# Denominators of layer 2 from pairs that GpSimd adds, and the row of maxima kept in PSUM

## The chip, the cores and the metric

The kernel runs on one core of one Trainium2 chip. The metric is the device time of one execution in microseconds (us); three runs of the kernel before took 3555.37 to 3556.21 us, median 3555.91. The engines are named as in the profile: PE is TensorE, DVE is VectorE, ACT is ScalarE, POOL is GpSimd, SP is SyncE.

## The reference

Three graph attention layers over 8192 nodes with 64 channels and one dense 0/1 adjacency matrix. Layer 0 attends over entity features, layers 1 and 2 over the features of the layer before. The core is the same in each:

```
scores = u[:, None] + v[None, :]            # one number per row, one per column
e      = where(adj > 0, leaky_relu(scores, 0.2), -9e15)
att    = softmax(e, axis=1)                 # exp(e - max), divided by its row sum
h      = elu(att @ features)
```

After layer 0 there is a residual sum and a layer norm; after layer 2 an output product over the concatenated features, a residual sum and a layer norm. So each of the 8192 x 8192 scores is made, masked, exponentiated, summed by row (the denominator) and multiplied with the features, three times over.

## The kernel before

Each layer runs over 16 blocks `b` of 512 rows. A block runs over 64 tiles `j` of 128 columns; a tile is 128 x 512 f32, with the graph's columns on the partitions. Four engines pass a tile on:

1. DVE `start_scores` (L1126) writes the score into one bank of `eps` in PSUM: `max(ua + v8, cb)`. `ua` is a row of the block, `cb` the row of maxima, both spread over the partitions in SBUF; `v8col` is one number per partition. This is called a fill below.
2. PE `mask_scores` (L736) adds -9e15 into the same bank where there is no edge. It splits the array by columns: two parts of 64 in layer 1 (`MASK_COLS`), four of 32 in layers 0 and 2, one of 128 beside other work. In layer 0 ACT fills some of the tiles.
3. ACT `probs` (L562) takes the exponential into one of 8 slots of `prob` in SBUF.
4. PE `main` (L780) adds features times probabilities of two tiles at once into bank `acc`. In layers 0 and 2 PE `denominators` (L789) also sums four tiles of `prob` at once, by a 128 x 32 matrix of ones each, into the four quarters of bank `den`. In layer 1 the denominator comes out of `acc` itself and there is no such product.

A fill of tile j waits for the exponential of the tile that had the bank: there are `ES` = 5 banks in turn. PSUM has 8 banks: five for `eps`, one each for `acc`, `den` and `misc`. `misc` takes everything else.

Every engine has its instructions in program order, written out by hand. In PE's loop over tiles the masks of `GROUP` tiles come first and then the sums of an earlier group (`LAG` groups back): 4 and 1 in layers 0 and 2, 2 and 2 in layer 1. At fixed tiles (`T_...`) stand the steps for other blocks. The tail of the block before: `T_EVAC`, `T_DEN` (ACT takes `acc` and `den` out), `T_TURN` (PE turns them), `T_A` (DVE divides), `T_EXP`, `T_B`, `T_HT`, `T_OUT`, `T_Y` (output sums and variances), `T_D` (result). The head of the next block: `T_XOR` (DVE makes edges, L974), `T_HIST` (PE counts them, L747), `T_FOLD`, `T_HEAD` (DVE finds the maxima, L992 to L1018), `T_HEADT`, `T_ROWS` (PE spreads them over the partitions in `misc`, ACT `rows_out` L623 copies them to `cb`), `T_UA` (DVE makes `ua`, L1132).

GpSimd has little to do: `tail` issues a power of -1/2 of four numbers per partition (L507, L517) and two DMAs a block (one in layer 2).

Of the kernel before, what the change touches and what calls it, by code (L numbers as in the profile page):

```python
# [46 lines left out]
GROUP = (QUAD, 2, QUAD)  # L47
LAG = (1, 2, 1)
TS = 2 * QUAD
ES = 5  # L50
AHEAD = 3
MASK_COLS = (32, 64, 32)
# [13 lines left out]
T_DEN = 5  # L66
T_TURN = 8
T_A = 13
T_EXP = 15
# [7 lines left out]
T_D = 40  # L77
# [24 lines left out]
def build(nc, x, adj, ent, W0, a0, W12, lin_w, lin_b, attn, mlp_w, mlp_b, out):  # L102
    with ExitStack() as ctx:
# [87 lines left out]
        eps = ps("eps", [P, ES, BI])  # L191
        acc = ps("acc", [P, BI])
        den = ps("den", [P, BI])
        misc = ps("misc", [P, BI])
        miscb = misc[:, :].bitcast(BF16)
# [46 lines left out]
        s_main = sem("probs_used")  # L242

# [51 lines left out]

        def freed(l, b, j):

            if j >= ES:
                return tile(l, b, j) - ES + 1
            last = max(i for i in range(NT) if i % ES == j)  # L300
            return tile(l, b, last) - NT + 1
# [181 lines left out]
        def _(pool):  # L483
# [20 lines left out]
            def tail(l, b):  # L504
                if l == 0:
                    pool.wait_ge(s_mom, blk(l, b) + 1)
                    nc.gpsimd.tensor_tensor(rstd[:, :], mom2[:, :], half[:, :], ALU.pow).then_inc(s_rstd, 1)  # L507
                if l < 2:

                    pool.wait_ge(s_oe, 4 * blk(l, b) + 4)  # L510
                    nc.gpsimd.dma_start(u_d[l + 1, bass.ds(b * BI, BI)].rearrange("(r p) -> r p", p=P),
                                        urow[:, :]).then_inc(s_ust, 16)
                    pool.wait_ge(s_y, blk(l, b) + 1)
                    nc.gpsimd.dma_start(xy_v[l, b], xin[:, :, :]).then_inc(s_x1, 16)
                else:
                    pool.wait_ge(s_mom2, b + 1)
                    nc.gpsimd.tensor_tensor(rstd[:, :], mom2[:, :], half[:, :], ALU.pow).then_inc(s_rstd2, 1)  # L517
                    pool.wait_ge(s_fin, b + 1)
                    nc.gpsimd.dma_start(out_v[b], pj[:, :, :]).then_inc(s_out, 16)

            for l in range(NLAYER):
                for b in range(NB):
                    tail(l, b)
# [3 lines left out]
        def _(act):  # L527
# [18 lines left out]
            def start_scores(l, b, j, par):  # L546

                if not (l == 0 and b == 0 and j < ES):
# [5 lines left out]
                nc.scalar.activation(eps[:, j % ES, :], ub[:, par, :], ACT.Relu, bias=v8col[:, j:j + 1],  # L554
                                     scale=1.0 - ALPHA).then_inc(s_filla, 1)

            def probs(l, b, j):

                if j % GROUP[l] == 0 and not (l == 0 and b == 0 and j < TS):
                    act.wait_ge(s_main, summed(l, b, j - TS + GROUP[l] - 1))  # L560
                act.wait_ge(s_z, tile(l, b, j) + 1)
                nc.scalar.activation(prob[:, j % TS, :], eps[:, j % ES, :], ACT.Exp,  # L562
                                     bias=v2col[:, j:j + 1]).then_inc(s_p, 1)

            def sums_out(l, b, par):
# [14 lines left out]
            def columns_out(l, b):  # L580
                act.wait_ge(s_htt, blk(l, b) + 1)
                nc.scalar.activation(ht[0:C, :], misc[0:C, :], ACT.Copy).then_inc(s_hte, 1)

            def products_out(l, b, i):

                act.wait_ge(s_om, 4 * blk(l, b) + i + 1)
                if i < 2:
                    v = misc[:, 0:2 * WC].rearrange("p (r w) -> p r w", w=WC)
# [19 lines left out]
                elif l < 2:  # L608

                    act.wait_ge(s_ust, 16 + 16 * blk(l, b))  # L610
                    nc.scalar.activation(urow[:, :], misc[0:RT, 0:P], ACT.Copy).then_inc(s_oe, 2)

            def counts_out(l, b):
                act.wait_ge(s_hist, MV * (blk(l, b) + 1))
                nc.scalar.activation(hs[:, :], misc[:, :], ACT.Copy).then_inc(s_hse, 1)  # L615

            def maxima_out(l, b, par):
                act.wait_ge(s_mt, blk(l, b) + 1)
                nc.scalar.activation(mrow[0:3, par, :], miscb[0:3, 0:BI], ACT.Copy).then_inc(s_mte, 1)  # L619
# [18 lines left out]
            for l in range(NLAYER):  # L638
                counts_out(l, 0)
                maxima_out(l, 0, 0)  # L640
                rows_out(l, 0, 0)

                def body(b, par, head, tail):
                    for t in range(NT):
# [8 lines left out]
                        if b == 0 and l == 1 and t == T_FSUM:  # L653
                            act.wait_ge(s_fs1, 1)
                            nc.scalar.activation(acc_s[0:C, 0:P], misc[0:C, 0:P], ACT.Copy).then_inc(s_fs1e, 1)
                        if b == 0 and t == T_FSUM + 4:
                            act.wait_ge(s_fsum, l + 1)
                            nc.scalar.activation(fsum[:, :], misc[:, 0:CE], ACT.Copy).then_inc(s_fsume, 1)
# [4 lines left out]
                        if head and t == T_ROWS:  # L663
# [9 lines left out]
        def _(pe):  # L673
# [9 lines left out]
            for i in range(ES):  # L683
# [40 lines left out]
            def mask_scores(l, b, j, par, cols):  # L724

                on_act = j in ON_ACT[l]
                et = eps[:, j % ES, :]
# [12 lines left out]
            def count_edges(l, b, m):  # L740
# [3 lines left out]
                for k in range(MT // 4):  # L744
                    for s in range(4):
                        j = 4 * k + s
                        mm = nc.tensor.matmul(misc[s * HB:(s + 1) * HB, :], oneh[:, m * MT + j, :],  # L747
# [5 lines left out]
            def turn_counts(l, b):  # L753
                pe.wait_ge(s_hse, blk(l, b) + 1)
                for r in range(RT):
                    mm = nc.tensor.matmul(misc[:, r * HB:(r + 1) * HB], hs[:, r * P:(r + 1) * P], fold[:, :],  # L756
# [3 lines left out]
            def feature_sum(l, j):  # L760
                if l == 1:
                    mm = nc.tensor.matmul(misc[0:C, 0:P], feat[:, 1, j, 0:C], ones[:, :], start=(j == 0),
# [4 lines left out]
                mm = nc.tensor.matmul(misc[:, 0:CE], ones[:, :], feat[:, l % 2, j, :], start=(j == 0),  # L767
# [495 lines left out]
```

## Time and profile before

| what | time |
|---|---|
| median of three runs | 3555.91 us |
| profiled execution, its own time | 3555.84 us |
| its span, first to last instruction | 3554.1 us |
| PE busy | 3220.6 us, 91% |
| DVE busy | 2877.7 us, 81% |
| ACT busy | 2261.3 us, 64% |
| POOL busy | 116.3 us, 3% |
| one block of layer 0, middle of the layer | 76.81 us |
| one block of layer 1 | 56.87 us |
| one block of layer 2 | 71.01 us |

The period of a block is the distance of two copies of `acc` (L570), which stand once in each block at the same tile. In the page's part 5 and in the grouped view, a row is a line of the kernel with its engine, operation, output and inputs, count, busy time and mean duration, and behind the second bar the idle time in front of it. Durations of consecutive instructions can overlap, so a count of instructions times their mean is more than their share of the time. One f32 matmul of the program stands as two records in the trace.

### The profile page before, as it was taken

The page shows a single profiled execution, that of the slowest core. Times are in us where ns is not written, and L with a number is a line of the kernel's source. Part 1 is how long each engine was busy: PE and PEld are TensorE (multiplying, and loading weights), DVE is VectorE, ACT ScalarE, POOL GpSimd, SP SyncE. Part 2 cuts the span into 40 slices and gives each one's busy share as a digit, 9 for nine tenths or more (in the row PEclk, how much of TensorE's full clock was granted, in tenths as well). Part 3 has the DMA queues.
Part 4 walks back from the last instruction along what each step waited for, and adds up shares of the span by engine and source line. Part 5 has one row for each costly group of instructions (what it writes and reads, how often), then busy time and mean ns, then how long its engine had stood idle before and what let it go on. Part 6 is the DMA issues. An engine that isn't in the chain of part 4 may idle for free. (4 is left out here: it accounts for less than half of the span.)

```text
span 3554.1 us, 60890 instructions
## 1 busy us (share of the span) xinstructions
PE 3220.6 (91%) x24158; PEld 1141.0 (32%) x24269; DVE 2877.7 (81%) x5283; ACT 2261.3 (64%) x3933; POOL 116.3 (3%) x138
## 2 busy tenths in 40 slices
PE   1579999999999997899999999979999999999998
PEld 0323333333333332333333333333333333333332
DVE  5468888888888875799999999976887888778876
ACT  0346666767766675577777877745656665666555
POOL 0000000000000000000000000000000000000000
PEclk9989999999999998999999999979999999999999
DMA  8999999999999941122212121211121112111200
GB/s 255 281 347 344 343 336 337 336 338 338 343 336 332 338 153 49 66 85 86 98 72 98 72 109 71 97 69 51 56 84 67 71 56 84 67 71 56 84 32 7
DMA packets 414127, 578.88 MB, mean 163 GB/s; under 512 B 294402, under 2 KB 315010, under 8 KB 389266
## 3 DMA queue, kind: packets, MB, share of 16 engines
q1 hardware_dynamic: 409458, 564.40, 49.4%
q0 software_dynamic: 4384, 10.59, 0.9%
q8 instruction: 190, 3.11, 0.3%
q14 instruction: 95, 0.78, 0.1%
HBM read 430.10 MB, written 77.69 MB: 143 GB/s over the span
## 5 line engine op out<-in xcount | busy, mean ns | idle before, releaser
L562 ACT ACTIVATE prob<-eps,v2col 128x512 f32<-128x512 f32 x3072 | 1945.5, 689 | 904.2 <-PE eps L736 894.8
L1126 DVE SCALAR_TENSOR_TENSOR eps<-ua,v8col,cb 128x512 f32<-128x512 f32 x2800 | 1975.6, 756 | 405.4 <-ACT prob L562 398.0
L780 PE MATMUL acc<-prob,feat 128*64 128x512 f32 x6144 | 1531.8, 605 | 6.7 <-ACT acc_s L570 6.7
L736 PE MATMUL eps<-nt,nbig 128*32 128x512 fp8e4 (+2 forms) x7852 | 964.6, 383 | 152.8 <-DVE eps L1126 136.3
L736 PEld LDWEIGHTS eps<-nt,nbig 128*32 128x32 bf16 (+2 forms) x7852 | 337.8, 100 | 866.9 <-DVE eps L1126 538.0
L780 PEld LDWEIGHTS acc<-prob,feat 128*64 128x64 f32 x6144 | 384.0, 136 | 596.1 <-issue 365.3
L789 PE MATMUL den<-prob,ones 128*32 128x512 f32 x4096 | 546.0, 605 | 0.0
L965 DVE TENSOR_SCALAR mi<-stage 128x1024 uint8<-128x1024 int32 x512 | 353.5, 692 | 66.3 <-DMA stage<-in_adj_dram 66.0
L974 DVE TENSOR_SCALAR edges<-nt 128x2048 int32<-128x2048 int32 x192 | 235.0, 1224 | 32.2 <-PE misc L747 16.8
L747 PE MATMUL misc<-edges,oneh 128*32 128x512 fp8e4 x3072 | 191.6, 392 | 70.6 <-DVE edges L974 55.8
L789 PEld LDWEIGHTS den<-prob,ones 128*32 128x32 f32 x4096 | 80.6, 108 | 417.7 <-issue 417.7
L554 ACT ACTIVATE eps<-ub,v8col 128x512 f32<-128x512 f32 x272 | 189.4, 696 | 0.0
L747 PEld LDWEIGHTS misc<-edges,oneh 128*32 128x32 bf16 x3072 | 85.4, 99 | 198.7 <-issue 81.6
L619 ACT ACTIVATE mrow<-misc 3x512 bf16<-3x512 bf16 x48 | 28.2, 587 | 110.9 <-PE misc L819 110.9
L733 PE MATMUL eps<-mrow,onesb 128*32 128x512 bf16 (+1 forms) x737 | 82.7, 379 | 8.7 <-ACT mrow L619 8.7
L615 ACT ACTIVATE hs<-misc 128x512 f32<-128x512 f32 x48 | 28.3, 590 | 94.6 <-PE misc L747 94.6
L856 PE MATMUL misc<-wcat,ht 65*128 65x130 f32 (+1 forms) x384 | 69.8, 306 | 6.5 <-ACT pj L606 4.5
L856 PEld LDWEIGHTS misc<-wcat,ht 65*128 65x128 f32 x384 | 52.5, 198 | 72.0 <-issue 37.3
L1041 DVE SCALAR_TENSOR_TENSOR g<-fsum,emp,misc 128x65 f32<-128x65 f32 x192 | 41.2, 278 | 29.1 <-PE misc L839 20.1
L756 PEld LDWEIGHTS misc<-fold,hs 128*128 128x128 f32 x384 | 47.3, 194 | 41.3 <-issue 36.5
L517 POOL TENSOR_TENSOR rstd<-mom,half 128x4 f32<-128x4 f32 x16 | 22.9, 1434 | 1106.5 <-DVE mom L1030 1106.5
L507 POOL TENSOR_TENSOR rstd<-mom,half 128x4 f32<-128x4 f32 x16 | 23.1, 1445 | 1096.8 <-DVE mom L1030 1096.8
(153 smaller groups left out, 1229.9 us busy)
## 6 DMA issues: line engine op xcount, KB each, us to landing
stage<-in_adj_dram SPq DMA_DIRECT2D x512, 512.0 KB, 6.6
nt<-nt_d SPq DMA_DIRECT2D x128, 1024.0 KB, 5.2
nt_d<-nt SPq DMA_DIRECT2D x64, 1024.0 KB, 7.2
ub<-u_d SPq DMA_DIRECT2D x48, 256.0 KB, 5.1
xy_d<-xin POOLq DMA_DIRECT2D x32, 256.0 KB, 3.2
xin<-xy_d SPq DMA_DIRECT2D x32, 256.0 KB, 2.9
nt<-mi SPq DMA_TRANSPOSE x256, 7.3
xin<-in_x_dram SPq DMA_DIRECT2D x16, 128.0 KB, 6.3
```

The lines of the kernel that those rows point to most:

```text
L554: nc.scalar.activation(eps[:, j % ES, :], ub[:, par, :], ACT.Relu, bias=v8col[:, j:j + 1], scale=1.0 - ALPHA).then_inc(s_filla, 1)
L562: nc.scalar.activation(prob[:, j % TS, :], eps[:, j % ES, :], ACT.Exp, bias=v2col[:, j:j + 1]).then_inc(s_p, 1)
L733: nc.tensor.matmul(et[c:c + cols, :], onesb[:, c:c + cols], mrow[:, par, :], start=False, stop=False, skip_group_check=True, tile_position ...
L736: mm = nc.tensor.matmul(et[c:c + cols, :], nbig[:, c:c + cols], edge, start=False, stop=True, skip_group_check=True, tile_position=(0, c))
L747: mm = nc.tensor.matmul(misc[s * HB:(s + 1) * HB, :], oneh[:, m * MT + j, :], half_block(edges[:, n % 2, :], m, j), start=(m == 0 and k == 0),
L756: mm = nc.tensor.matmul(misc[:, r * HB:(r + 1) * HB], hs[:, r * P:(r + 1) * P], fold[:, :], start=True, stop=True)
L780: mm = nc.tensor.matmul(acc[h:h + C, :], feat[:, l % 2, j, 0:C], prob[:, j % TS, :], start=(k == 0), stop=(k == NT // 2 - 1))
L789: mm = nc.tensor.matmul(den[32 * i:32 * i + 32, :], ones[:, 0:32], prob[:, (QUAD * k + i) % TS, :], start=(k == 0), stop=(k == NT // QUAD ...
L856: mm = nc.tensor.matmul(misc[:, r * WC + w:(r + 1) * WC], ht[:, (2 * i + r) * P:(2 * i + r + 1) * P], wcat[:, l, w:WC], start=True, stop=True)
L965: dv.tensor_scalar(out, src, 0, ONE8, ALU.is_le, ALU.mult).then_inc(s_mask, 1)
L974: dv.tensor_scalar(edges[:, n % 2, :].bitcast(I32), nt[:, b % 2, m, :].bitcast(I32), EDGE_FLIP, None, ALU.bitwise_xor).then_inc(s_xor, 1)
L1126: dv.scalar_tensor_tensor(eps[:, j % ES, :], ua[:, par, :], v8col[:, j:j + 1], cb[:, par, :], ALU.add, ALU.max).then_inc(s_fill, 1)
```

## The change

In layer 2 GpSimd adds the probabilities of tiles 2p and 2p+1 into one of eight slots `pairs`, which lie in `stage`, a buffer that only layer 0 uses. PE's new `pair_sums` sums four such pairs at once, so once in 8 tiles where `denominators` ran once in 4. `GROUP`, `LAG` and `MASK_COLS` of layer 2 become those of layer 1. `probs` in layer 2 also waits for GpSimd's sum of the slot's former tiles.

The bank of `den` is now bank 5 of `eps`. In layers 1 and 2 the rows of maxima stay in PSUM, in `misc` for even blocks and in bank 4 of `eps` for odd ones; all work on block b that stood in `misc` stands in that bank (`max_bank`, `work_bank`). `rows_out` remains in layer 0 only, and fills and `ua` read the maxima from PSUM. So the fills have five banks in turn in layers 0 and 1 (in layer 1 bank 5 in place of 4) and four in layer 2. Four tail steps of all layers stand one tile later, the result of layer 2 six tiles later.

```diff
-GROUP = (QUAD, 2, QUAD)
-LAG = (1, 2, 1)
+GROUP = (QUAD, 2, 2)
+LAG = (1, 2, 2)
+PS = 8
+DLAG = 5
-ES = 5
+SLOTS = ((0, 1, 2, 3, 4), (0, 1, 2, 3, 5), (0, 1, 2, 3))
-MASK_COLS = (32, 64, 32)
+MASK_COLS = (32, 64, 64)
-T_DEN = 5
-T_TURN = 8
-T_A = 13
-T_EXP = 15
+T_DEN = 6
+T_TURN = 9
+T_A = 14
+T_EXP = 16
-T_D = 40
+T_D = 46
+P_RSTD = 18
+P_OUT = 24
...
+        def max_bank(l, b):
+            return (misc[:, :], eps[:, 4, :])[b % 2]
+        def work_bank(l, b):
+            return misc[:, :] if l == 0 else max_bank(l, b + 1)
...
+            def pair_sum(b, p):
+                q = b * NT // 2 + p
+                if q >= PS and q % QUAD == 0:
+                    pool.wait_ge(s_den, (q - PS) // QUAD + 1)
+                pool.wait_ge(s_p, tile(2, b, 2 * p + 1) + 1)
+                nc.gpsimd.tensor_tensor(pairs[:, q % PS, :], prob[:, 2 * p % TS, :], prob[:, (2 * p + 1) % TS, :],
+                                        ALU.add).then_inc(s_psum, 1)
...
                     act.wait_ge(s_main, summed(l, b, j - TS + GROUP[l] - 1))
+                    if l == 2 and (b or j >= TS):
+                        act.wait_ge(s_psum, (b * NT + j - TS) // 2 + 1)
...
+            def pair_sums(b, g):
+                pe.wait_ge(s_psum, (b * NT // 2) + QUAD * (g + 1))
+                if g == 0:
+                    pe.wait_ge(s_dene, den_blocks(2, b))
+                for i in range(QUAD):
+                    mm = nc.tensor.matmul(den[32 * i:32 * i + 32, :], ones[:, 0:32], pairs[:, (QUAD * g + i) % PS, :],
+                                          start=(g == 0), stop=(g == NT // PS - 1))
+                mm.then_inc(s_den, 1)
...
+                        if l == 2 and t % PS == DLAG:
+                            g = t // PS - 1
+                            if g >= 0:
+                                pair_sums(b, g)
+                            elif tail:
+                                pair_sums(b - 1, NT // PS + g)
...
-                dv.scalar_tensor_tensor(eps[:, j % ES, :], ua[:, par, :], v8col[:, j:j + 1], cb[:, par, :],
+                dv.scalar_tensor_tensor(bank(l, j), ua[:, par, :], v8col[:, j:j + 1], maxima(l, b, par),
                                         ALU.add, ALU.max).then_inc(s_fill, 1)
```

On PE, in a plain stretch of layer 2 before (`nbig` is the mask, `feat` the features, `ones` the matrix of ones), one group of four tiles stands so:

```order
L736 MATMUL eps<-nt,nbig 32x512 [waits scores_started_by_dve]
L736 MATMUL eps<-nt,nbig 32x512 x3
L736 MATMUL eps<-nt,nbig 32x512 [waits scores_started_by_dve]
L736 MATMUL eps<-nt,nbig 32x512 x3
L780 MATMUL acc<-prob,feat 64x512 [waits probs_done] x4
L789 MATMUL den<-prob,ones 32x512 x4
```

Two of its four masks are left out here, which read alike. And now, around the place where the pair sums stand (`stage` holds the pairs, `eps` is also the bank of the denominators):

```order
L785 MATMUL eps<-nt,nbig 64x512 [waits scores_started_by_dve]
L785 MATMUL eps<-nt,nbig 64x512
L829 MATMUL acc<-prob,feat 64x512 [waits probs_done] x2
L848 MATMUL eps<-stage,ones 32x512 [waits pairs_summed_by_pool]
L848 MATMUL eps<-stage,ones 32x512 x3
```

Each group is now two tiles, the four matmuls with `ones` follow every fourth group, and they wait for GpSimd and no longer stand behind the probabilities alone. On GpSimd, layer 2 had only the power and the DMA of the result. In the changed kernel one stretch of a block around them reads:

```order
L550 TENSOR_TENSOR stage<-prob 128x512 [waits probs_done] x2
L538 TENSOR_TENSOR rstd<-mom,half 128x4 [waits last_variance_done]
L550 TENSOR_TENSOR stage<-prob 128x512 [waits probs_done]
L550 TENSOR_TENSOR stage<-prob 128x512 [waits probs_done,pair_sums_used]
L550 TENSOR_TENSOR stage<-prob 128x512 [waits probs_done] x3
L550 TENSOR_TENSOR stage<-prob 128x512 [waits probs_done,pair_sums_used]
L542 DMA out_dram<-pj 128x4x64 [waits result_done]
```

The 32 sums of a block are new, and the two old steps stand between them, behind pair 18 and pair 24.

## Rows read from the trace of the kernel before

**Rows 1.** Windows: one block each of layers 1 and 2 (busy us and count per engine, PEclk).

```profile
1962.43:2019.30 56.87, 53.25 (x341) 19.09 (x340) 53.99 (x96) 44.14 (x78) 1.28 (x2) 1.00 0.24 90
2903.32:2974.33 71.01, 69.11 (x560) 23.18 (x563) 57.11 (x108) 42.93 (x73) 2.75 (x2) 1.00 0.19 70
```

**Rows 2.** Timeline of ACT: the copies of `acc` (start, us, ...).

```profile
1962.43 0.60 ACT L570 ACTIVATE acc_s<-acc 128x512 f32<-128x512 f32 x1
...
2019.30 0.60 ACT L570 ACTIVATE acc_s<-acc 128x512 f32<-128x512 f32 x1
...
2903.32 0.60 ACT L570 ACTIVATE acc_s<-acc 128x512 f32<-128x512 f32 x1
...
2974.33 0.60 ACT L570 ACTIVATE acc_s<-acc 128x512 f32<-128x512 f32 x1
```

**Rows 3.** Chain that ended last, layer 2: one plain group (start, us, what).

```profile
2912.54 1.00 PE den L789 x8
2913.53 0.86 PE eps L736 x16
2914.40 1.87 PE acc L780 x8
```

**Rows 4.** The same chain where the next block's maxima are made.

```profile
2952.49 1.02 PE misc L756 x8
...
2959.56 0.40 PE eps L736 x4
...
2963.50 0.60 ACT mrow L619
2964.10 0.27 issue
```

**Rows 5.** Timeline of PE in layer 1: the masks of three consecutive groups.

```profile
2047.50 0.62 PE L736 MATMUL eps<-nt,nbig 128*64 128x512 fp8e4 x4
...
2048.82 0.60 PE L736 MATMUL eps<-nt,nbig 128*64 128x512 fp8e4 x4
...
2050.11 0.60 PE L736 MATMUL eps<-nt,nbig 128*64 128x512 fp8e4 x4
```

**Rows 6.** Timeline of layer 2: from mask to exponential, fill, and GpSimd.

```profile
2904.09 1.05 PE L736 MATMUL eps<-nt,nbig 128*32 128x512 fp8e4 x16
2904.59 0.69 ACT L562 ACTIVATE prob<-eps,v2col 128x512 f32<-128x512 f32 x1 [0.67 <-PE eps L736]
...
2908.42 0.69 ACT L562 ACTIVATE prob<-eps,v2col 128x512 f32<-128x512 f32 x1 [0.92 <-PE eps L736]
...
2909.14 0.76 DVE L1126 SCALAR_TENSOR_TENSOR eps<-ua,v8col,cb 128x512 f32<-128x512 f32 x1 [0.68 <-ACT prob L562]
...
2910.04 0.86 DVE L1041 SCALAR_TENSOR_TENSOR g<-fsum,emp,misc 128x65 f32<-128x65 f32 x4
...
2934.93 3.40 DVE L1126 SCALAR_TENSOR_TENSOR eps<-ua,v8col,cb 128x512 f32<-128x512 f32 x5
...
2935.10 1.46 POOL L517 TENSOR_TENSOR rstd<-mom,half 128x4 f32<-128x4 f32 x1 [65.87 <-DVE mom L1030]
```

**Rows 7.** Grouped view of DVE, the same block of layer 2.

```profile
L1126 DVE SCALAR_TENSOR_TENSOR eps<-ua,v8col,cb 128x512 f32<-128x512 f32 x65 | 45.4, 755 | 11.8 <-ACT prob L562 11.8
L974 DVE TENSOR_SCALAR edges<-nt 128x2048 int32<-128x2048 int32 x4 | 4.9, 1222 | 0.0
L1041 DVE SCALAR_TENSOR_TENSOR g<-fsum,emp,misc 128x65 f32<-128x65 f32 x4 | 0.9, 276 | 0.1
L1132 DVE SCALAR_TENSOR_TENSOR ua<-ub,cb 128x512 f32<-128x512 f32 x1 | 0.7, 687 | 0.0
```

**Rows 8.** Grouped view of GpSimd over the span: one operation at two sizes.

```profile
L496 POOL TENSOR_SCALAR_AFFINE_SELECT halves<-halves 128x64 f32<-128x64 f32 x2 | 0.5, 237 | 0.1
...
L492 POOL TENSOR_SCALAR_AFFINE_SELECT ident<-ident 128x128 f32<-128x128 f32 x1 | 0.3, 289 | 0.2 <-POOL halves L489 0.2
```

**Rows 9.** Timeline of the start of layer 2.

```profile
2386.88 0.60 ACT L623 ACTIVATE cb<-misc 128x512 f32<-128x512 f32 x1 [0.70 <-remote]
2387.51 0.69 DVE L1132 SCALAR_TENSOR_TENSOR ua<-ub,cb 128x512 f32<-128x512 f32 x1 [2.59 <-ACT cb L623]
```

More of the change, by code:

```diff
@@ L294, in landed, with bank @@
             return s_mload[b % 2 * MV + m], 16 * ((l - 1) * (NB // 2) + b // 2 + 1)
-        def freed(l, b, j):
-            if j >= ES:
-                return tile(l, b, j) - ES + 1
-            last = max(i for i in range(NT) if i % ES == j)
+        def bank(l, j):
+            return eps[:, SLOTS[l][j % len(SLOTS[l])], :]
+        def max_bank(l, b):
+            return (misc[:, :], eps[:, 4, :])[b % 2]
+        def work_bank(l, b):
+            return misc[:, :] if l == 0 else max_bank(l, b + 1)
+        def freed(l, b, j):
+            n = len(SLOTS[l])
+            if j >= n:
+                return tile(l, b, j) - n + 1
+            if b == 0:
+                return tile(l, 0, 0)
+            last = max(i for i in range(NT) if i % n == j)
             return tile(l, b, last) - NT + 1
@@ L521, in _, with first_rstd, rows_stored @@
-            for l in range(NLAYER):
-                for b in range(NB):
-                    tail(l, b)
+            def first_rstd(b):
+                pool.wait_ge(s_mom, b + 1)
+                nc.gpsimd.tensor_tensor(rstd[:, :], mom2[:, :], half[:, :], ALU.pow).then_inc(s_rstd, 1)
+            def rows_stored(l, b):
+                pool.wait_ge(s_oe, 4 * blk(l, b) + 4)
+                nc.gpsimd.dma_start(u_d[l + 1, bass.ds(b * BI, BI)].rearrange("(r p) -> r p", p=P),
+                                    urow[:, :]).then_inc(s_ust, 16)
+                pool.wait_ge(s_y, blk(l, b) + 1)
+                nc.gpsimd.dma_start(xy_v[l, b], xin[:, :, :]).then_inc(s_x1, 16)
@@ new lines, in _ @@
+            for b in range(NB):
+                first_rstd(b)
+                rows_stored(0, b)
+            for b in range(NB):
+                rows_stored(1, b)
+            for b in range(NB):
+                for p in range(NT // 2):
+                    pair_sum(b, p)
+                    if b > 0 and p == P_RSTD:
+                        last_rstd(b - 1)
+                    if b > 0 and p == P_OUT:
+                        result_stored(b - 1)
+            last_rstd(NB - 1)
+            result_stored(NB - 1)
@@ L546, in start_scores @@
             def start_scores(l, b, j, par):
-                if not (l == 0 and b == 0 and j < ES):
+                if not (l == 0 and b == 0 and j < len(SLOTS[0])):
                     act.wait_ge(s_p, freed(l, b, j))
@@ L553, in start_scores @@
                     act.wait_ge(s_ub[par], ub_count(l, b, par))
-                nc.scalar.activation(eps[:, j % ES, :], ub[:, par, :], ACT.Relu, bias=v8col[:, j:j + 1],
+                nc.scalar.activation(bank(l, j), ub[:, par, :], ACT.Relu, bias=v8col[:, j:j + 1],
                                      scale=1.0 - ALPHA).then_inc(s_filla, 1)
@@ L640, in _ @@
                 maxima_out(l, 0, 0)
-                rows_out(l, 0, 0)
+                if l == 0:
+                    rows_out(l, 0, 0)
                 def body(b, par, head, tail):
@@ L681, in _ @@
                 nc.tensor.transpose(misc[0:C, 0:C], wld[:, l, :], ident[0:C, 0:C]).then_inc(s_wt, 1)
-            for i in range(ES):
+            for i in SLOTS[0]:
                 for r in range(RT):
@@ L726, in mask_scores @@
                 on_act = j in ON_ACT[l]
-                et = eps[:, j % ES, :]
+                et = bank(l, j)
                 m, o = divmod(j, MT)
@@ L823, in spread_maxima @@
                 pe.wait_ge(s_mte, blk(l, b) + 1)
-                nc.tensor.matmul(misc[:, :], onesb[:, :], mrow[:, par, :], start=True, stop=True).then_inc(s_cb, 1)
+                nc.tensor.matmul(work_bank(l, b - 1), onesb[:, :], mrow[:, par, :], start=True, stop=True).then_inc(s_cb, 1)
             def tail_step(l, b, t):
+                wb = work_bank(l, b + 1)
                 if t == T_TURN:
@@ L1118, in tail_step, with maxima @@
                     tail_result(b)
+            def maxima(l, b, par):
+                return cb[:, par, :] if l == 0 else max_bank(l, b)
             def start_scores(l, b, j, par):
-                if not (l == 0 and b == 0 and j < ES):
+                if not (l == 0 and b == 0 and j < len(SLOTS[0])):
                     dve.wait_ge(s_p, freed(l, b, j))
```

104 lines of the change are left out of this document (54 added, 50 removed).

## The prediction

> **What bounds the kernel now.** I read the page's shares first, then cut the span into blocks by the copies of `acc` and read one block of layer 1 and one of layer 2 in the windows view, then followed the chain that ended last through the block of layer 2, and at last looked in the timeline for the single distances. A block of layer 1 takes 2019.30 - 1962.43 = 56.87 us, one of layer 2 2974.33 - 2903.32 = 71.01 [rows 2]. In layer 2 PE is busy 69.11 of the 71.01 us and DVE 57.11; in layer 1 it is 53.25 and 53.99 of 56.87 [rows 1]. So layer 2 is bound by PE, and layer 1 by PE and DVE in turn, with DVE a little ahead.
>
> The chain shows what PE's time in layer 2 is made of: a plain group of four tiles is 1.00 (denominators) + 0.86 (masks) + 1.87 (features) = 3.73 us [rows 3], sixteen groups 59.7. The other 11.3 us of the block hold two stalls, at the maxima. The chain leaves PE at 2952.49 + 1.02 = 2953.51 and comes back at 2959.56 [rows 4]; in these 6.05 us PE did one group (3.73) and one mask (about 0.4), so about 1.9 were lost. Further on PE waits for `mrow`, 0.60 + 0.27 [rows 4]. That is 2.8 us of stalls, and 8.5 of other work (edge counts, turning, products).
>
> **The change, part by part.** The sum is made against the profiled execution, 3555.84 us (span 3554.1), which stands 0.07 below the median of the runs.
>
> PE alone. Masks and features go in groups of two tiles, as in layer 1. There three consecutive groups start at 2047.50, 2048.82 and 2050.11 [rows 5], so one takes 2.61 / 2 = 1.305 us and 32 take 41.8. Denominators: 8 times 1.00 in place of 16 [rows 3]. With the 8.5 of other work PE needs 41.8 + 8.0 + 8.5 = 58.3 us per block. Before, it needed 59.7 + 8.5 = 68.2.
>
> DVE alone. It keeps every instruction, so it needs what it was busy, at most 57.1 us [rows 1]. The two engines are now within 1.2 us of each other, and what counts is how well they go on beside each other.
>
> The loop over four banks. A first mask of a group starts at time 0. Its exponential starts 0.50 later (2904.59 - 2904.09) and takes 0.69; the next of the pair ends about 0.6 later, at 1.8. A fill starts 0.03 after the exponential that frees its bank (2909.14 against 2908.42 + 0.69) and takes 0.76; fills in a row are (3.40 - 0.76) / 4 = 0.66 apart [rows 6]. So the fills of tiles 4 and 5 end at 1.98 and 2.64. Their masks are due at 2 x 1.305 = 2.61 and 2.82. The second has a slack of under 0.2 us. With five banks each fill could have started a tile earlier. So plain stretches just hold, and whatever DVE does between the fills (four makings of edges of 1.22 [rows 7], the division, the features, the output's variances, the maxima; about eight separate places) makes PE wait, unless PE itself is in a denominator or other work then.
>
> Size of it. Layer 1 has this rhythm of groups with five banks and no denominators, and takes 56.87. To that come: the output of layer 2 on DVE, where DVE is busy 57.11 - 53.99 = 3.1 us more, of which I put 1.2 down to a dozen more fills that stand singly and read 0.76 for 0.66 (an estimate), so 1.9; eight denominators, each between 0 (DVE was behind and catches up) and 1.00 (DVE is held by the banks and stops too); one bank less, between 0 and 8 x 0.66 = 5.3. That gives 58.8 to 72.1 us. I take the middle, 65.4, because the denominators fall at tiles 5, 13, 21, ... and DVE's insertions at others, about half of them within reach, and because the slack of 0.2 says that the missing bank is felt but that neighbouring insertions share one wait. Gain per block 71.0 - 65.4 = 5.6, for 16 blocks 90 us.
>
> GpSimd's sums. No row shows an addition of two 128x512 tiles. One operation with one input takes 237 ns for 64 columns and 289 for 128 [rows 8], 0.81 ns per column, so 0.19 + 0.42 = 0.60 us for 512. That is the lower end. If the second input is read after the first, 1.02. The upper end puts the 1.46 us of the power of four numbers [rows 6] under it, 2.5. I take 1.0: the program reads two tiles. 32 of them and the 2.75 us that POOL does now [rows 1] are 35 of the 65 us, so they are hidden; a pair is needed by PE five tiles after its last exponential and by ACT some six tiles after. The cover is gone when a sum takes over (65.4 - 2.75) / 32 = 1.96 us. On GpSimd the power waits behind pair 18 for a variance that DVE makes at tile 35, and the DMA behind pair 24 for a result of tile 46; both are past when GpSimd comes there, so the pairs behind them are not held. The Trainium skill (GPSIMD Engine Reference, section 3.1 Elementwise) gives 4497 ns for such an addition of 2048 columns; a quarter is 1.12 us, an estimate from that page, and the sum would stay as it is.
>
> Fills from PSUM. Their second tile input moves to PSUM, which no fill of before shows. Four of the small operations with an input in PSUM take 0.86 us together and one 0.28 [rows 6, 7], so they are 0.19 apart for 65 columns. Fills are 0.66 apart for 512. Together that is (0.66 - 0.19) / 447 = 1.05 ns per column, and 0.12 to 0.13 us fixed on either, though one reads PSUM and the other does not; so the input in PSUM costs nothing in the distance. The other reading is by duration: 276 ns for 65 columns against 687 for 512 from SBUF alone [rows 7]; with 1.05 per column the fixed parts are 208 and 149, so 59 ns dearer. The ends are 0 and +0.06 per fill (below nothing I see -0.01, were the shared part cheaper). I take 0, since DVE is paced by distances.
>
> Small parts. `rows_out` goes from ACT, 0.60 us a block, and ACT is busy 43 of 71 us: nothing. At the start of layers 1 and 2 it stood between PE and `ua`, 2387.51 - 2386.88 = 0.63 [rows 9]: 1.3 us gained in both together. The tail steps one tile later and bank 5 for 4 in layer 1 cost nothing: each step keeps its order. At the end of the program GpSimd's last sum (1.0) lies beside the last features (two groups, 1.87): nothing. Sum: 3555.8 - 90 - 1.3 = 3464.5, so 3465 us.
>
> **Rivals.**
>
> Dens hidden (A): DVE uses every denominator to catch up and the fourth bank suffices. For it: DVE lags in layer 1 all the time. Against it: the slack of 0.2. The block takes 60 and the time is 3555.8 - 1.3 - 16 x 11.0 = 3378; halfway, 62.5, it is 3418.
>
> Shared port (B): GpSimd reads SBUF for 32 x 1.0 = 32 us of a block, half the time, and DVE's instructions that read two SBUF inputs or run double wait for it. In rows 6 five fills with two SBUF inputs take 3.40 us while the power runs, at their usual distance, but that reads four numbers only. Some 20 instructions of DVE per block (edges, tail, maxima) that each wait a quarter of a microsecond are 5 us on an engine without slack: block 70.4, time 3544. The Trainium skill (SBUF — State Buffer, section Who interferes with whom) says that a DVE instruction with two SBUF inputs or in a two-port mode contends with a GpSimd instruction that reads SBUF, and that the second to come is blocked wholly; a fill with its maxima in PSUM has one SBUF input and is free. By it the fills stay at 0.66 and the tail instructions stretch. No row here shows a collision, so the rule keeps its share below.
>
> Fills slower (C), the rival on the other side: a fill that both reads and writes PSUM is 0.06 us further apart. Place: every fill of layers 1 and 2. DVE leads in layer 1, so 64 x 0.06 = 3.8 us a block there, and as much in layer 2, where both are tight: 32 x 3.8 = 122, time 3465 + 122 = 3587. It decides from 90 / 2048 = 0.044 us per fill on. Against it: the distance of the small operations.
>
> Sums too long (D): one takes 2.5 us; a block takes 32 x 2.5 + 2.75 = 82.8, time 3555.8 + 16 x 11.8 = 3743. For it only the upper bound.
>
> **Chances.** Forecast (block of 63 to 68.5, 3425 to 3515) 0.53; A 0.17; B 0.13; C 0.10; D 0.03; no change, since stalls eat all, 0.04. I predict 3465 us. The range 3400 to 3565 leaves out the better part of A and C and D, under 0.2 together; the forecast's own range is 3425 to 3515. A measurement of this kernel tells 0.2%, 7 us, from no change. Faster: 0.53 + 0.17 + most of B 0.09 = 0.79; within 0.2%: 0.06; slower 0.15.
>
> **What would show it.** A block of layer 1 at 56.5 to 57.3 and fills at their 0.66 distance (else C). A block of layer 2 at 65.4, with PE busy about 60 us and waiting for fills some 5 to 7 us, right behind DVE's insertions; if DVE waits for exponentials less than 2 us per block, A. GpSimd's sums at 1.0 us and busy half the time (else D), PE and ACT not waiting for them; edges over 1.22 us and fills unchanged mean B. I am wrong on the size if PE's waits in plain stretches are not near zero, for then the loop over four banks is longer than reckoned.

## The result, and the profile after

The changed kernel takes 3598.84 us (median of four runs, 3596.43 to 3600.11), the kernel before 3556.06 in the same comparison: a ratio of 1.012, 95% interval 1.0102 to 1.0137. It is slower by 43 us, 1.2%, where 91 us less had been forecast. The profiled execution has a span of 3596.9 us against 3554.1.

Windows of one block of layer 1 and one of layer 2 after the change (as [rows 1]; busy us and count of PE, PEld, DVE, ACT, POOL, then PEclk):

```profile
1951.82:2007.72 55.90, 52.85 (x342) 19.34 (x338) 53.70 (x96) 43.60 (x78) 1.28 (x2) 1.00 0.25 89
2836.56:2911.78 75.22, 64.29 (x415) 20.91 (x411) 65.14 (x108) 43.85 (x74) 45.20 (x35) 0.98 0.18 66
```

The timeline of ACT has the copies of `acc` that answer to [rows 2], here one block of layer 2 apart:

```profile
2761.48 0.60 ACT L615 ACTIVATE acc_s<-acc 128x512 f32<-128x512 f32 x1
...
2836.56 0.60 ACT L615 ACTIVATE acc_s<-acc 128x512 f32<-128x512 f32 x1
```

A block of layer 1 fell from 56.87 to 55.90 us. A block of layer 2 did not fall from 71.0 to 65.4 but rose to 75.1. From the copies: layer 2, first to last copy, 1056.6 us before and 1115.3 after, +58.7; all that lies in front of it -16. Together that is the 43 us.

In layer 2 PE is busy 5 us less than before, as meant, but DVE is busy 65.1 of 75.2 us against 57.1, with the same 108 instructions. The grouped view of DVE says which of them grew (the block from 2761.48; compare [rows 7]):

```profile
L1200 DVE SCALAR_TENSOR_TENSOR eps<-ua,v8col,eps 128x512 f32<-128x512 f32 x58 | 40.5, 748 | 8.9 <-ACT prob L607 8.8
L1042 DVE TENSOR_SCALAR edges<-nt 128x2048 int32<-128x2048 int32 x4 | 6.3, 1574 | 0.0
...
L1073 DVE SCALAR_TENSOR_TENSOR nm<-vucol,nm 128x4 f32<-128x4 f32 x1 | 1.8, 1810 | 0.0
...
L1138 DVE SCALAR_TENSOR_TENSOR hn<-hn,z 128x256 f32<-128x256 f32 x1 | 1.4, 1368 | 0.0
...
L1068 DVE SCALAR_TENSOR_TENSOR ns<-vm,gst,vucol 128x4 f32<-128x4 f32 x1 | 1.1, 1150 | 0.0
```

Two of the same instructions before, in the grouped view of DVE for its block of layer 2:

```profile
L1069 DVE SCALAR_TENSOR_TENSOR hn<-hn,z 128x256 f32<-128x256 f32 x1 | 0.4, 426 | 0.0
...
L1005 DVE SCALAR_TENSOR_TENSOR nm<-vucol,nm 128x4 f32<-128x4 f32 x1 | 0.2, 161 | 0.0
```

The fills, which now read one tile from PSUM, kept their 0.75 us. An instruction on four numbers per partition (L1073) took 1.81 us, where it had taken 0.16. The timeline shows beside what. First the division `z`, then the maxima of the next block:

```profile
2772.01 1.28 POOL L550 TENSOR_TENSOR stage<-prob 128x512 f32<-128x512 f32 x1 [0.17 <-ACT prob L607]
2772.23 1.34 DVE L1118 TENSOR_TENSOR z<-g,rden 128x256 f32<-128x256 f32 x1
...
2815.93 1.27 POOL L550 TENSOR_TENSOR stage<-prob 128x512 f32<-128x512 f32 x1 [1.09 <-ACT prob L607]
...
2816.07 1.15 DVE L1068 SCALAR_TENSOR_TENSOR ns<-vm,gst,vucol 128x4 f32<-128x4 f32 x1
2817.14 0.79 POOL L542 DMA_DIRECT2D out_dram<-pj  x1
...
2817.45 1.81 DVE L1073 SCALAR_TENSOR_TENSOR nm<-vucol,nm 128x4 f32<-128x4 f32 x1
2817.96 1.27 POOL L550 TENSOR_TENSOR stage<-prob 128x512 f32<-128x512 f32 x1
```

A sum on GpSimd starts, a DVE instruction with two inputs in SBUF starts into it, and DVE ends only when GpSimd has ended: L1068 at 2817.22 against 2817.20; `z`, which still has its 256 columns to do, ends 0.28 later. L1073 ends with its sum too, at 2819.26 against 2819.23, but it had started 0.51 us before that sum, while GpSimd issued a DMA. Behind that, on PE (timeline), and the granted clock around it (windows):

```profile
2820.11 0.41 PE L785 MATMUL eps<-nt,nbig 128*64 128x512 fp8e4 x2 [3.19 <-DVE eps L1200]
...
2821.60 1.92 PE L829 MATMUL acc<-prob,feat 128*64 128x512 f32 x4
...
2825.32 1.02 PE L829 MATMUL acc<-prob,feat 128*64 128x512 f32 x4
```

```profile
2811.00:2816.00 5.00, 5.00 (x36) 2.12 (x30) 3.97 (x10) 3.14 (x7) 2.61 (x3) 1.00 0.50 170
2816.00:2820.00 4.00, 0.92 (x6) 0.04 (x2) 3.86 (x6) 1.23 (x2) 3.20 (x3) 1.00 0.27 86
2820.00:2825.00 5.00, 4.24 (x18) 0.92 (x20) 4.08 (x11) 1.37 (x2) 1.27 (x1) 0.66 0.00 0
```

PE, busy 0.92 of 4 us, waited 3.19 us for a fill. Then the granted clock fell from 1.00 (2.4 GHz) towards half (1.2 GHz), a mean of 0.66 over 5 us, and four feature matmuls took 1.92 us that take 1.02 a little later.

GpSimd itself is no bound. Its sums take 1.33 us on the mean, and it waits 29.6 us of the block for exponentials (grouped view and waits of the same block):

```profile
L550 POOL TENSOR_TENSOR stage<-prob 128x512 f32<-128x512 f32 x33 | 43.8, 1331 | 30.0 <-ACT prob L607 29.6
```

```profile
POOL stage L550 <- ACT prob L607: 29.6, 23, 3.4
...
PEld eps L848 <- POOL stage L550: 0.8, 1, 0.8
```

### The profile page after: what moved, and what is told of

It reads as the page before. It is cut to its first block and busy times, and to the rows that moved or that the text cites. A ratio compares the mean times of both kernels' runs of the same rounds, so it can differ in the third digit from the quotient of the medians.

```text
span 3596.9 us, 57223 instructions
## 1 busy us (share of the span) xinstructions
PE 3146.0 (87%) x21935; PEld 1109.9 (31%) x21935; DVE 2993.9 (83%) x5283; ACT 2266.6 (63%) x3901; POOL 792.8 (22%) x650
## 5 line engine op out<-in xcount | busy, mean ns | idle before, releaser
L785 PE MATMUL eps<-nt,nbig 128*64 128x512 fp8e4 (+2 forms) x6542 | 1006.9, 386 | 262.6 <-DVE eps L1200 261.1
L1200 DVE SCALAR_TENSOR_TENSOR eps<-ua,v8col,misc 128x512 f32<-128x512 f32 x1024 | 707.1, 749 | 123.0 <-ACT prob L607 120.3
L550 POOL TENSOR_TENSOR stage<-prob 128x512 f32<-128x512 f32 x512 | 678.5, 1329 | 510.1 <-ACT prob L607 505.5
L1200 DVE SCALAR_TENSOR_TENSOR eps<-ua,v8col,eps 128x512 f32<-128x512 f32 x1024 | 702.9, 749 | 88.1 <-ACT prob L607 86.0
L1200 DVE SCALAR_TENSOR_TENSOR eps<-ua,v8col,cb 128x512 f32<-128x512 f32 x752 | 557.2, 755 | 148.0 <-ACT prob L607 146.7
L785 PEld LDWEIGHTS eps<-nt,nbig 128*64 128x64 bf16 (+2 forms) x6542 | 328.4, 104 | 1115.2 <-DVE eps L1200 801.8
L838 PE MATMUL eps<-prob,ones 128*32 128x512 f32 x2048 | 273.1, 605 | 0.0
L796 PE MATMUL misc<-edges,oneh 128*32 128x512 fp8e4 x2048 | 129.3, 395 | 71.4 <-DVE edges L1042 56.7
L848 PE MATMUL eps<-stage,ones 128*32 128x512 f32 x1024 | 143.0, 632 | 0.0
L796 PE MATMUL eps<-edges,oneh 128*32 128x512 fp8e4 x1024 | 61.1, 380 | 0.0
```

What stands on the lines that cost most here:

```text
L550: nc.gpsimd.tensor_tensor(pairs[:, q % PS, :], prob[:, 2 * p % TS, :], prob[:, (2 * p + 1) % TS, :], ALU.add).then_inc(s_psum, 1)
L785: mm = nc.tensor.matmul(et[c:c + cols, :], nbig[:, c:c + cols], edge, start=False, stop=True, skip_group_check=True, tile_position=(0, c))
L796: mm = nc.tensor.matmul(work_bank(l, b - 1)[s * HB:(s + 1) * HB, :], oneh[:, m * MT + j, :], half_block(edges[:, n % 2, :], m, j), start=( ...
L838: mm = nc.tensor.matmul(den[32 * i:32 * i + 32, :], ones[:, 0:32], prob[:, (QUAD * k + i) % TS, :], start=(k == 0), stop=(k == NT // QUAD ...
L848: mm = nc.tensor.matmul(den[32 * i:32 * i + 32, :], ones[:, 0:32], pairs[:, (QUAD * g + i) % PS, :], start=(g == 0), stop=(g == NT // PS - 1))
L1200: dv.scalar_tensor_tensor(bank(l, j), ua[:, par, :], v8col[:, j:j + 1], maxima(l, b, par), ALU.add, ALU.max).then_inc(s_fill, 1)
```

## The experiments

Two theories stood against each other. P, the port: DVE instructions with two SBUF inputs (or at double rate) stand still while GpSimd reads. R, the ring: four banks and groups of two are too short for what DVE does between the fills. All rows below are windows of one block of layer 2 unless said otherwise. Four runs of the changed kernel lie within 3.7 us, so a smaller difference in time is not read where only one run was made; the lengths of neighbouring blocks, which in most of these kernels agree within 0.1 us, are.

**GpSimd writes only.**

```diff
-                nc.gpsimd.tensor_tensor(pairs[...], prob[...], prob[...], ALU.add).then_inc(s_psum, 1)
+                nc.gpsimd.memset(pairs[:, q % PS, :], 2.0).then_inc(s_psum, 1)
```

> The changed kernel, but GpSimd fills each pair slot with a constant (it only writes) and reads no probabilities; the denominators of layer 2 are therefore not computed. Waits, banks and PE's work stay. Theory P (port: DVE instructions with two SBUF inputs or at double rate stand still while GpSimd reads): DVE busy per block of layer 2 falls from 65.1 to about 57 us, edges from 1.57 to 1.22 us, and the block from 75.1 to about 67 us, time about 3470 us. Theory R (ring: four banks and groups of two are too short, the port does not matter for the time): DVE's instructions get shorter, but the block stays at 73 to 75 us, time about 3580 us.

Measured: 3467.8 us (one run; before 3558.6 on the same chip).

```profile
2722.48:2788.98 66.50, 62.22 (x414) 20.91 (x411) 57.34 (x108) 43.67 (x74) 20.81 (x34) 1.00 0.20 73
```

DVE is back at 57.3 and the block at 66.5 us. P holds: that GpSimd reads costs 75.1 - 66.5 = 8.6 us a block. The times are also what the forecast had been made for, 65.4 and 3465. GpSimd's instructions are shorter too when they only write, but that is not the cause: in the block read above PE waited for the sums only 0.8 us. Writing alone is not quite free: one conversion of four numbers beside it takes 0.57 us, where it took 0.17 before (grouped view).

```profile
L1079 DVE CAST parts<-nm 128x4 bf16<-128x4 f32 x1 | 0.6, 565 | 0.0
```

**Five banks, rows of maxima in SBUF, sums on GpSimd.**

```diff
-SLOTS = ((0, 1, 2, 3, 4), (0, 1, 2, 3, 5), (0, 1, 2, 3))
+SLOTS = ((0, 1, 2, 3, 4), (0, 1, 2, 3, 5), (0, 1, 2, 3, 4))
...
-            return misc[:, :] if l == 0 else max_bank(l, b + 1)
+            return misc[:, :] if l != 1 else max_bank(l, b + 1)
...
-                return cb[:, par, :] if l == 0 else max_bank(l, b)
+                return cb[:, par, :] if l != 1 else max_bank(l, b)
```

> The changed kernel with layer 2's rows of maxima in SBUF again and five banks of scores (layer 1 stays changed); GpSimd adds the pairs. P: now the fills too have two SBUF inputs and stand still during sums; with GpSimd reading 43 of 75 us, fills grow from 0.75 us to 1.0 or more and the block from 75 to 85 us or more, time over 3700 us. R: the fifth bank gives its slack back, the block falls to about 70 us, time about 3520 us.

Measured: 3860.8 us (one run). The window, and the fills in the grouped view of DVE:

```profile
2746.17:2838.63 92.46, 69.98 (x412) 21.49 (x411) 87.29 (x108) 45.07 (x75) 53.89 (x35) 0.91 0.15 53
```

```profile
L1200 DVE SCALAR_TENSOR_TENSOR eps<-ua,v8col,cb 128x512 f32<-128x512 f32 x65 | 66.1, 1078 | 4.5 <-ACT prob L607 4.4
```

A fill with its second tile in SBUF takes 1.08 us on the mean beside the sums, with the same tile in PSUM 0.75. R alone would have given 70. So the rows of maxima had to go to PSUM if GpSimd was to add in this way, and that took the fifth bank.

**Five banks, GpSimd writes only** (the two edits above together).

> As the kernel with five banks and rows in SBUF in layer 2, but GpSimd only writes constants (denominators of layer 2 not computed). Against the four-bank kernel with the same write-only GpSimd it gives the price of the bank. P alone: both blocks equal within 1 us, about 66. R: the five banks are 4 to 6 us per block faster, about 61 to 62 us, time about 3385 us. I expect 62.

Measured: 3433.4 us (one run).

```profile
2840.18:2904.62 64.44, 61.68 (x412) 21.01 (x409) 57.16 (x108) 43.60 (x74) 21.58 (x34) 1.00 0.20 76
```

The fifth bank, with the rows of maxima back in SBUF, is worth 66.5 - 64.4 = 2.1 us a block, less than R said. The rows' copy on ACT is back too, so the bank alone may be worth more; no run parts the two in layer 2.

**The kernel before with four banks in layer 2.**

```diff
-ES = 5
+ESL = (5, 5, 4)
...
-eps[:, j % ES, :]
+eps[:, j % ESL[l], :]
```

> The kernel before with four banks in turn in layer 2 in place of five, nothing else. R: groups of four tiles need four banks at once, so PE's masks wait for fills behind every group: the block grows from 71.0 to 75 us or more, time 3620 us or more. P says nothing of it: 71 to 72 us, time 3560 us.

Measured: 3616.5 us (one run).

```profile
2780.04:2855.06 75.02, 70.21 (x560) 23.07 (x563) 57.08 (x108) 43.08 (x73) 2.61 (x2) 1.00 0.17 66
```

In groups of four the missing bank costs 4.0 us a block, in groups of two 2.1 with the copy gone in exchange. That fits shorter groups needing fewer banks, though the two pairs of kernels also differ in their denominators.

**Only layer 1 changed, with the steps at their old tiles, and with the later ones.** Layer 2 as before, from the changed kernel:

```diff
-GROUP = (QUAD, 2, 2)
-LAG = (1, 2, 2)
-MASK_COLS = (32, 64, 64)
+GROUP = (QUAD, 2, QUAD)
+LAG = (1, 2, 1)
+MASK_COLS = (32, 64, 32)
...
-                    pair_sum(b, p)
-                        if l == 2 and t % PS == DLAG:
...
-T_TURN = 9
+T_TURN = 8
```

> Only layer 1 changed: its rows of maxima stay in PSUM, in two banks in turn, bank 5 in place of 4. Layers 0 and 2 as before (rows in SBUF, five banks, groups of four and denominators by PE in layer 2), and all steps at the tiles of before. In the changed kernel a block of layer 1 took 55.90 against 56.87 us. If the rows in PSUM did it (no copy on ACT in front of exponentials at the block's end), layer 1 keeps 55.9 and the time is 3555.9 - 15 - 1 = 3540 us. If the later tail steps did it, the block is 56.9 and the time 3556.

> As the kernel with only layer 1 changed, but with the changed kernel's later tail steps in all layers. If the steps' places matter, it differs by 5 us or more from the other; I expect the same within 3 us, 3540 us, and a block of layer 1 of 55.9 in both.

Measured: 3541.36 us, ratio 0.996 (0.9945 to 0.9974), and 3539.2 with the later steps (one run). Windows of a block of layer 1 and one of layer 2 of the first:

```profile
1953.91:2009.82 55.91, 52.85 (x342) 19.20 (x338) 53.72 (x96) 43.75 (x78) 1.28 (x2) 1.00 0.25 90
2817.66:2888.91 71.25, 69.32 (x561) 23.17 (x563) 57.09 (x108) 42.90 (x73) 2.75 (x2) 1.00 0.18 69
```

The second block is the longest of its layer; the others take 71.00 us, as before. The change of layer 1 gives 0.97 us a block; the later steps give nothing there, as the blocks with either are equal to 0.02 us. The timelines of DVE, before and then after, show most of it:

```profile
2013.03 1.42 DVE L1126 SCALAR_TENSOR_TENSOR eps<-ua,v8col,cb 128x512 f32<-128x512 f32 x2 [0.88 <-ACT prob L562]
```

```profile
1947.58 4.71 DVE L1200 SCALAR_TENSOR_TENSOR eps<-ua,v8col,eps 128x512 f32<-128x512 f32 x7 [0.17 <-ACT prob L607]
```

Near the end of a block DVE stood 0.88 us for an exponential; without the 0.60 us copy in front of it on ACT it stands 0.17. That is 0.7 of the 0.97 us. The rest fits DVE's busy time, 53.99 us before [rows 1] and 53.72 now.

**Groups of two in layer 2, denominators by PE.** From the kernel with only layer 1 changed and the later steps, groups of two in layer 2 as well:

```diff
+                if l == 2:
+                    main(l, b, k)
+                    if k % 2 == 1:
+                        denominators(l, b, k // 2)
```

> Layer 1 changed; in layer 2 five banks and rows in SBUF, but groups of two tiles and two masks of 64 columns, with PE's denominators of four tiles behind every second group and no sums on GpSimd. PE needs 41.8 + 16 x 1.0 + 8.5 = 66.3 us per block where it needed 68.2. R (the rhythm of two costs stalls at DVE's insertions only, five banks hold it): block 67.5 to 69, time 3540 - 16 x 2.8 = 3495 us. If the rhythm itself costs, block 71 or more, time 3540 or more.

Measured: 3528.96 us, ratio 0.9924 (0.9909 to 0.9939).

```profile
2881.18:2951.32 70.14, 69.43 (x477) 22.82 (x476) 57.19 (x108) 44.04 (x74) 2.25 (x2) 1.00 0.19 70
```

A gain of 0.87 us a block, under a third of the 2.8 expected. Its chain of waits shows it: a mask group behind denominators stands with 0.55 us, not 0.43, so four tiles take 3.70 us where 3.61 had been reckoned, and before 3.73 [rows 3].

```profile
2820.65 0.55 PE eps L779 x4
2821.20 0.86 PE acc L823 x4
2822.06 0.43 PE eps L779 x4
2822.49 0.86 PE acc L823 x4
2823.35 1.00 PE eps L832 x8
```

**Each sum in four instructions.**

```diff
+                for c in range(4):
+                    ins = nc.gpsimd.tensor_tensor(pairs[:, q % PS, c * 128:(c + 1) * 128], ..., ALU.add)
+                ins.then_inc(s_psum, 1)
```

> The changed kernel with each of GpSimd's sums in four instructions of 128 columns. P in the form 'DVE waits to the end of the GpSimd instruction that runs': a wait is at most a quarter as long, so DVE's busy time per block falls from 65.1 to about 60 us and the block to about 69 us, time about 3505 us, if GpSimd's four pieces take under 1.9 us together. P in the form 'DVE gets in only when GpSimd has nothing left': DVE is as long or longer, the block 75 us or more. If each piece costs half a microsecond or more, GpSimd itself bounds the block: 32 x 2.2 = 70 us and more.

Measured: 3568.7 us (one run). The window, and GpSimd in the grouped view:

```profile
2748.57:2821.31 72.74, 64.34 (x415) 20.99 (x411) 62.15 (x108) 43.74 (x74) 60.61 (x131) 0.98 0.19 67
```

```profile
L551 POOL TENSOR_TENSOR stage<-prob 128x128 f32<-128x128 f32 x129 | 58.4, 488 | 12.1 <-ACT prob L610 12.1
```

DVE's busy time falls by 3 us, though GpSimd reads for longer in all. So the length of the one instruction that DVE runs into counts; DVE gets in between two of them in most places. Not in all: the conversion L1083, four numbers per partition, took 1.35 us, the time of three pieces. Blocks took 72.7 and 74.0 us in turn, a gain of 1.1 to 2.4 us where 6 were expected: a piece takes 0.45 us alone and 0.49 on the mean, not a quarter of 1.33, so GpSimd was at work for 60.6 of 72.7 us, in which DVE can meet it.

**GpSimd reads one input.**

```diff
-                nc.gpsimd.tensor_tensor(pairs[...], prob[...], prob[...], ALU.add).then_inc(s_psum, 1)
+                nc.gpsimd.tensor_scalar(pairs[...], prob[:, 2 * p % TS, :], 0.5, None, ALU.add).then_inc(s_psum, 1)
```

> The changed kernel with GpSimd adding a constant to one tile of the pair, so that it reads one input and not two (the denominators of layer 2 are therefore not the sums). By the small GpSimd operations with one input it should take about 0.7 us in place of 1.33. P: what counts is how long GpSimd reads: half as often and half as long a wait, so of the 8.6 us per block between the write-only kernel (66.5) and the changed one (75.1) a quarter to a half remains: block 68.5 to 70.5 us, time about 3515 us. If only a GpSimd instruction with two inputs stops DVE, the block is 66.5 and the time 3468.

Measured: 3509.5 us (one run), blocks of 68.8 to 70.4 us. The time is as expected, the duration is not (grouped views of GpSimd and DVE):

```profile
L550 POOL TENSOR_SCALAR stage<-prob 128x512 f32<-128x512 f32 x32 | 50.1, 1578 | 16.9 <-ACT prob L606 16.6 <-issue 0.2
```

```profile
L1041 DVE TENSOR_SCALAR edges<-nt 128x2048 int32<-128x2048 int32 x4 | 4.9, 1217 | 0.0
```

It takes 1.58 us on the mean, longer than the sum of two tiles, and costs DVE less: edges are not stretched, 1.22 against 1.57, though smaller instructions still are. But edges do meet it, and there GpSimd is the one that is held, though it had started first (timelines of GpSimd and DVE):

```profile
2743.55 1.49 POOL L550 TENSOR_SCALAR stage<-prob 128x512 f32<-128x512 f32 x1 [0.91 <-ACT prob L606]
...
2767.59 2.29 POOL L550 TENSOR_SCALAR stage<-prob 128x512 f32<-128x512 f32 x1 [1.81 <-ACT prob L606]
```

```profile
2768.20 1.21 DVE L1041 TENSOR_SCALAR edges<-nt 128x2048 int32<-128x2048 int32 x1
```

How long GpSimd runs is therefore not the whole measure; an instruction of it that reads two tiles holds DVE more than one that reads one. Why, and which DVE instruction is held by which, is left open.

**Sums only where DVE does little but fills.**

```diff
+                if p // QUAD in (0, 6, 7):
                     nc.gpsimd.tensor_tensor(...)
+                else:
+                    nc.gpsimd.memset(pairs[:, q % PS, :], 2.0).then_inc(s_psum, 1)
```

> The changed kernel with GpSimd adding only the pairs of tiles 0 to 7 and 48 to 63 of each block of layer 2 and writing constants for the others (their denominators are left out). P: DVE does nothing but fills for most of the time in which these sums run (its insertions stand at tiles 14 to 53, and it is about five tiles ahead), so little is left of the 8.6 us: block 67 to 68.5 us, time about 3490 us. If instead fills suffered from the sums, 3/8 of the price stays and more: block 69.7 us or more.

Measured: 3528.0 us (one run), a miss: blocks of 69.9, 70.4 and 71.4 us in turn. The window of one of the longest, that of the stretch behind its maxima, and two DVE groups:

```profile
2741.37:2812.74 71.37, 65.20 (x415) 21.37 (x411) 59.60 (x108) 43.61 (x73) 29.97 (x35) 0.95 0.18 68
```

```profile
2795.00:2802.00 7.00, 6.38 (x24) 1.45 (x24) 4.29 (x12) 2.21 (x4) 1.27 (x1) 0.52 0.00 0
```

```profile
L1076 DVE SCALAR_TENSOR_TENSOR nm<-vucol,nm 128x4 f32<-128x4 f32 x1 | 1.8, 1807 | 0.0
L1071 DVE SCALAR_TENSOR_TENSOR ns<-vm,gst,vucol 128x4 f32<-128x4 f32 x1 | 1.3, 1254 | 0.0
```

The sum of pair 24 and the one behind it still met two instructions of the maxima. DVE was busy 2.3 us longer than without reads, but this block took 4.9 us more: the rest fits the clock, which was at 0.52 for 7 us behind the stall.

**The same with those two pairs left out.**

```diff
-                if p // QUAD in (0, 6, 7):
+                if p < 4 or p >= 26:
```

> As the kernel in which GpSimd adds only the pairs of tiles 0 to 7 and 48 to 63, but the pairs of tiles 48 to 51 are written as constants too, so sums run in tiles 0 to 7 and 52 to 63 only. There two DVE instructions of the maxima (four numbers per partition) took 1.25 and 1.81 us in place of 0.22 and 0.16, PE stood for over 3 us and then ran at a granted clock of 0.52 for 7 us; the block was 71.4 against 66.5 us. P with the clock: both go, the block is 66.5 to 67.2, the granted clock 1.00, time 3468 to 3480 us, though 10 of the 12 sums remain and run beside fills. If the sums beside fills cost something, or the late clock has another cause, the block stays at 69 or more.

Measured: 3465.3 us (one run). Window, and the sums:

```profile
2720.00:2786.48 66.48, 62.21 (x414) 20.90 (x411) 57.30 (x108) 43.62 (x73) 28.48 (x35) 1.00 0.21 75
```

```profile
L551 POOL TENSOR_TENSOR stage<-prob 128x512 f32<-128x512 f32 x11 | 14.0, 1274 | 8.3 <-ACT prob L610 8.0
```

Fourteen us of sums beside fills cost nothing, to 0.02 us. Two sums at the wrong place had cost 4.9 us in the block shown, and (3528.0 - 3465.3) / 16 = 3.9 us on the mean.

**Groups of two in layer 0 too.**

```diff
-GROUP = (QUAD, 2, 2)
+GROUP = (2, 2, 2)
...
-                if l == 2:
+                if l != 1:
```

> The best version so far (rows in PSUM in layer 1, groups of two with denominators by PE in layer 2, no sums on GpSimd, 3529 us) with groups of two and masks of 64 columns in layer 0 as well. In layer 2 the rhythm gave 0.87 us per block; layer 0 is bound by PE as layer 2 was and has 16 blocks: 10 to 20 us less, 3510 to 3520 us. If the making of masks on DVE (512 instructions of 0.69 us) makes PE wait more in the shorter rhythm, no gain or a loss: 3529 us or more.

Measured: 3501.84 us, ratio 0.9849 (0.9833 to 0.9866), the fastest kernel here that computes everything. A block of layer 0, whose length now changes from block to block, 73.8 to 75.8 us in the middle of the layer:

```profile
472.75:548.09 75.34, 73.35 (x507) 24.36 (x507) 65.36 (x125) 54.45 (x95) 3.31 (x3) 1.00 1.11 346
```

Layer 0 gains 1 to 3 us a block (76.81 before), 27 us in all against the kernel with groups of two in layer 2 alone, where 10 to 20 were expected.

## Why the prediction was wrong

The step that failed is the one of DVE: "It keeps every instruction, so it needs what it was busy, at most 57.1 us". It needed 65.1, because its instructions wait for GpSimd's reads of SBUF. The prediction had that as rival B, "Shared port", and went wrong in its chance and its price: it gave it 0.13 and 5 us a block, with "No row here shows a collision". It was the case, at 8.6. The sign that the prediction named for it, edges over 1.22 us and fills unchanged, is what came. By the runs, a block of layer 2 goes

| step | us | forecast |
|---|---|---|
| before | 71.0 | |
| groups of two, five banks, PE's denominators | 70.1 (-0.9) | -1.9 for PE alone |
| 8 denominators fewer, GpSimd writes only | 64.4 (-5.7) | -8.0 to 0 |
| four banks, rows of maxima in PSUM | 66.5 (+2.1) | 0 to +5.3 |
| GpSimd reads | 75.1 (+8.6) | 0, in rival B +5 |

The size of B was too small for two reasons. It let some 20 instructions wait a quarter of a microsecond each; in truth about a dozen of a block wait, most to the end of a GpSimd instruction of 1.3 us, however short they are, together 65.1 - 57.3 = 7.8 us of busy time. By the mean durations in the grouped views of before and after, those with two SBUF inputs grew by 6.6 us in all, the edges by 1.4 and one scaling of four numbers (L1093) by 0.5. And it had no term for the clock: a stall of 3 us on PE is followed by matmuls at half speed. What each of the two takes of the 8.6 us no run tells.

The chance was wrong because the row against B could not speak on it. The five fills beside the power of four numbers [rows 6] had two SBUF inputs and were not stretched, but that GpSimd instruction reads next to nothing. A row that does not contain the thing is no evidence that the thing does not happen.

The rule of the Trainium skill (SBUF — State Buffer, section Who interferes with whom) spoke against the change and was put beside the sum. On what contends with what, the runs agree with it: fills with one SBUF input free (0.75 us), with two blocked (1.08), writes alone all but harmless to DVE (57.3 us). It also says that whoever issues first keeps the ports for its whole instruction and the other waits. Many rows fit that, but not the instruction of 1.81 us, which had started 0.51 us before its sum, nor the edges that started 0.61 us into a GpSimd instruction with one input and held it up. There the measurements decide, and the order is left open.

What held. The block without the port came out at 66.5 for 65.4, and the time at 3467.8 for 3465. That the times lie within 3 us is partly luck: layer 2 gave 16 x 4.5 = 72 us of the 90, and layer 1 gave 14 that had been put at nothing. And 65.4 was the middle of a span from 58.8 to 72.1. Fills from PSUM (C) were the same, 0.75 us, so the price by distance was right and the one by duration was not. A sum took 1.33 us where 1.0 was taken and 1.96 was the limit (D). Neither ACT nor PE waited for GpSimd to speak of, 0.8 us. A was ruled out by the 2.1 us of the bank and by 64.4 us even with five.

What was costed at nothing and was not: the copy of the maxima on ACT in layer 1, 0.7 us a block, and with the shorter work of DVE 0.97, which is 14 us over the layer. ACT as a whole had room, but this one copy stood in front of exponentials that DVE waited for. The start of the layers gave its 1 us or so, as said.

PE's own need was put too low by about 3 us a block: with all denominators and five banks it is busy 69.4 of 70.1 us, where 66.3 had been reckoned. The masks behind denominators take 0.12 us longer than in layer 1, which has none, and sixteen times 3.70 for 3.61 is 1.4 us. Another 0.9 was read wrongly: the prediction took 2.8 us of the block before for stalls, but PE was idle for only 71.01 - 69.11 = 1.9 us of it [rows 1]. At the maxima it was idle 6.05 - 4.73 = 1.3 us and not 1.9, and for `mrow` 0.58 and not 0.87 (window and timeline of PE, before). The last 0.8 us was not taken apart.

```profile
2953.51:2959.56 6.05, 4.73 (x32) 1.15 (x30) 5.61 (x19) 3.99 (x7) 0.00 (x0) 1.00 0.05 20
```

```profile
2964.37 0.59 PE L736 MATMUL eps<-nt,nbig 128*128 128x512 fp8e4 x2 [0.58 <-ACT mrow L619]
```

## What to carry to other kernels

Before work goes to an idle GpSimd, list the instructions that DVE runs at that time and count those with two SBUF inputs (here the edges, with one, grew too, from 1.22 to 1.57 us): each can wait a whole GpSimd instruction, so short GpSimd instructions, a PSUM input on DVE's side, or another place in the block decide it. A trace that has no GpSimd reads says nothing on this; one run with GpSimd only writing gives the price at once. And a copy on an engine with room is not free if it stands in front of an instruction that others wait for.

## What the runs showed of the hardware

Not expected: a DVE instruction on 4 numbers per partition took 1.81 us beside a GpSimd sum of 1.27 us, longer than the sum; it had started while GpSimd was still issuing the DMA in front of it. In the kernel where GpSimd only writes, the same instruction inside the same DMA issue took 0.16 us, so the issue alone does not hold it. Four sums of 128 columns take 1.7 to 1.9 us against 1.27 for one of 512. A GpSimd addition of a constant to one tile took 1.49 us alone, more than that of two tiles, and left edges at 1.22 us, but was itself stretched to between 1.7 and 2.6 us where they met. A stall of PE of 3.2 us was followed by 5 to 7 us at a granted clock of 0.66 and 0.52.
